# Turning gathered expert rows by a transposing DMA and a joining copy on ScalarE, in place of TensorE's transposes

## The chip, the cores and the metric

The kernel runs on one core of one Trainium2 chip. The metric is the device time of one execution in microseconds (us). Instructions run on TensorE (PE), VectorE (DVE), ScalarE (ACT) and GpSimd (POOL); SyncE (SP) issues most of the transfers, POOL and, after the change, ACT issue some too. All transfers run on the core's 16 DMA engines, whoever issues them.

## The reference

Eight sequences of 100 tokens (800 tokens of 512 words, float32) pass through a gated cross-attention block and then a gated mixture-of-experts block:

```
x = x + tanh(g_xattn) * attention(layernorm(x), ctx)          # 16 heads, fake-quantised q, k, v, weights
x = x + tanh(g_ffn)   * moe(layernorm(x))

moe(x): scores = softmax(x @ Wg.T)                            # 16 experts in 4 groups
        keep 2 groups, then 4 experts of them, with their scores as weights
        h_e = silu(x @ W1_e.T) * (x @ W3_e.T)                  # 352 wide
        y   = sum over the 4 chosen experts of score * h_e @ W2_e.T
        z   = the same product with 2 shared experts
        return y + z
```

The change touches only how the rows of one expert are brought into the layout that `x @ W1_e.T` and `x @ W3_e.T` need. Everything there is float32.

## The kernel before, in words

**Order of the work.** Projections and quantisation come first (to about 220 us), then 100 attention tiles (to about 604 us), the output projection with the second layer norm and the routing logits (to 644 us), and then the mixture of experts, 48 steps of 128 token rows. The first nine steps (`PRE`) and the last five (`POST`) are steps of the two shared experts, whose rows lie transposed in SBUF already (`x2_t`). Between them lies a loop of 17 pairs, 34 routed steps, each with one 128-row tile of the tokens of one expert.

**How the routed rows travel.** The normed tokens lie in `xn` (128 tokens by 512 words for each of T = 7 tiles). While PE is in the first shared steps, DVE ranks the experts and works out for each token four slots in a DRAM buffer, `expert_in`. POOL then scatters the tokens into their slots with 28 indirect transfers (line 1465), waits for all of them, and loads the first two tiles. In the loop POOL loads tile s + 2 into one of two buffers, `x_rows[:, q]` (line 1471), when that buffer has been read, and stores tile s - 2's result from `y_rows` to `expert_out` (line 1475) when DVE has copied it from PSUM. At the end each token gathers its four results.

**One routed step s on PE** (`routed` in the tensor block), in its order: wait for the expert's weights, for `s_xec` (this tile's rows are turned) and for `s_hm`; the first up product, four matmuls for W1, which the trace shows as eight passes (`up`, line 746); transposes of the previous step's hidden rows (`transpose_hidden`, line 757); the second up product for W3 (line 746), which ends in `s_h`; the transposes of the next tile's rows, s + 1 (`transpose_rows`, line 776); the down product of the previous step (`down`, line 766).

**The same step on ACT** (`routed` in the scalar block): `copy_hidden` moves the previous step's transposed hidden rows from PSUM to SBUF (line 968, PE's down product waits for it), `silu` on the first up product (line 962, DVE's gate at line 1284 waits for it), `copy_rows` moves the transposed rows of tile s + 1 to `xe_t` (line 974), which PE's next step waits for. DVE multiplies the two halves of the hidden rows (line 1284) and copies the down product to `y_rows` (line 1302).

**Weights.** Two transfers per expert, 1408 KB and 768 KB, are issued by SP (lines 493 and 494) into a ring of three slots, as soon as PE's down product of an expert's last tile has ended. Other than these SP issues nothing in the loop. No engine but SP issues a transposing transfer in this kernel; the ones there are, of 128 rows by 1536 half words (line 467) and of 128 by 2048 (line 410), belong to the attention part.

Of the kernel before, what the change touches and what calls it, by code (L numbers as in the profile page):

```python
# [7 lines left out]
def gated_xattn_moe_kernel(  # L8
# [16 lines left out]
    f32, bf16, i16 = mybir.dt.float32, mybir.dt.bfloat16, mybir.dt.int16  # L25
    u8, u16 = mybir.dt.uint8, mybir.dt.uint16
    ALU, ACT, AX = mybir.AluOpType, mybir.ActivationFunctionType, mybir.AxisListType

    P = 128
    NTOK, D = x.shape  # L30
    DC = D // P
# [4 lines left out]
    T = (NTOK + P - 1) // P  # L36
# [15 lines left out]
    MAXT = (NTOK * TOPK - E) // P + E + 1  # L52
# [7 lines left out]
    def shared_step(u):  # L60

        if u < PRE - T:
            return 0, u
        return (1, u - (PRE - T)) if u < PRE else (0, u - T)
# [22 lines left out]
    with ctx:  # L87
        def sb(name, shape, dt):
            return ctx.enter_context(nc.sbuf_tensor(name, shape, dt))

        def sem(name):
            return ctx.enter_context(nc.semaphore(name))
# [2 lines left out]
        key_parts = nc.dram_tensor("key_parts", [KPAD, H * P], bf16, kind="Internal").ap()  # L95


        expert_in = nc.dram_tensor("expert_in", [(MAXT + 1) * P, D], f32, kind="Internal").ap()
        expert_out = nc.dram_tensor("expert_out", [(MAXT + 1) * P, D], f32, kind="Internal").ap()


# [9 lines left out]
        xt = sb("xt", [P, T * D], f32)  # L111
# [7 lines left out]
        ident = sb("ident", [P, P], f32)  # L119
# [58 lines left out]
        ps = ctx.enter_context(nc.psum_tensor("ps", [P, 8, BANK], f32))  # L178
# [34 lines left out]
        def slot_for(n):  # L213
            return 0 if n == 0 else 1 + (n - 1) % RING

        x_rows = xt[:, 0:2 * D].rearrange("p (b d) -> p b d", b=2)
        xe_t = xt[:, 2 * D:4 * D].rearrange("p (b k q) -> p b k q", b=2, k=DC)
        y_rows = xt[:, 4 * D:6 * D].rearrange("p (b d) -> p b d", b=2)

        xn = arena_b[:, 0:T * D].rearrange("p (t d) -> p t d", t=T)  # L220
# [4 lines left out]
        v_fs = [v_f, xt[:, 0:KPAD]]  # L225

        x_t = xt[:, :].rearrange("p (k q) -> p k q", k=DC)
        attn = xt[:, :].rearrange("p (t d) -> p t d", t=T)

        zero_tile = xt[:, KPAD:KPAD + D]  # L230
# [30 lines left out]
        s_xn = sem("normed_ready")  # L261
# [52 lines left out]
        s_xz = sem("expert_in_zeroed")  # L314
        s_scat = [sem(f"tokens_scattered_{j}") for j in range(TOPK)]
        s_win = [sem(f"weights_in_{i}") for i in range(RING + 1)]
        s_wready = sem("expert_weights_ready")
        s_xr = [sem("expert_rows_in_0"), sem("expert_rows_in_1")]
        s_xtr = sem("expert_rows_transposes_done")
        s_xec = sem("expert_rows_transposed_copied")  # L320
        s_h = sem("up_products_done")
        s_silu = sem("silu_done")
# [16 lines left out]
        def rows_in(s, q):  # L339

            return 16 * (s // 2 + 1) if isinstance(s, int) else (s - q) * 8 + 16
# [27 lines left out]
        def tile_place(n):  # L369

            if n >= LAST:
                return LAST_PLACES[n - LAST]
            g, r = divmod(n, GT)
            return (g, None, T - 1) if r == GT - 1 else (g, g * HG + r // (T - 1), r % (T - 1))
# [11 lines left out]
        def _(sp):  # L386
            for t in range(T):
                rows = P if t < T - 1 else TAIL
# [14 lines left out]
            for i, a in enumerate(range(0, NKEY, CTX_PIECE)):  # L403
                b = min(a + CTX_PIECE, NKEY)
# [25 lines left out]
            def transpose_values(g):  # L430

                sp.wait_ge(s_vb, g + 1)
                sp.dma_start_transpose(v_q[:, :, g * P:(g + 1) * P], v_b).then_inc(s_vq, 16)
# [3 lines left out]
            for kt in range(KT):  # L437
                sp.wait_ge(s_parts, kt + 1)
                if kt < 2:
                    sp.wait_ge(s_fourth, kt + 1)  # L440
                sp.dma_start(key_parts[kt * P:(kt + 1) * P, :],
                             parts[:, (T + kt) % 2].rearrange("p h g d -> p (h g d)")).then_inc(s_kp[(T + kt) % 2], 16)
                if kt == 0:
                    sp.wait_ge(s_ztile, 1)
                for rows, a in ZEROED[len(ZEROED) * kt // KT:len(ZEROED) * (kt + 1) // KT]:
                    sp.dma_start(rows[a * P:(a + 1) * P, :], zero_tile).then_inc(s_xz, 16)
                if kt in GROUP_AT and kt < KT - 1:
                    transpose_values(GROUP_AT[kt])
            sp.wait_ge(s_kp[T % 2], 16 * ((KT + 1) // 2))
# [20 lines left out]
            for n in range(NTILE):  # L470
                g, head, t = tile_place(n)
# [52 lines left out]
            for t in range(T):  # L524
                rows = P if t < T - 1 else TAIL
# [6 lines left out]
        def _(pe):  # L532
# [210 lines left out]
            def up(src, col, q, w):  # L743

                for k in range(DC):
                    last = mm(ps[:, 1 + 2 * q + w, 0:INTER], src(k),  # L746
                              arena_a[:, bass.ds(col + (w * DC + k) * INTER, INTER)],
                              start=(k == 0), stop=(k == DC - 1))
                return last
# [17 lines left out]
                              arena_a[0:IW[c], bass.ds(col + UPC + c * D, D)], start=(c == 0), stop=(c == IC - 1))  # L767
                last.then_inc(s_y, 1)

            def transpose_rows(s, q):  # L770

                pe.wait_ge(s_xr[q], rows_in(s, q))
                if not isinstance(s, int) or s >= 1:
                    pe.wait_ge(s_xec, s)
                for k in range(DC):
                    last = nc.tensor.transpose(ps[:, 0, k * P:(k + 1) * P], x_rows[:, q, k * P:(k + 1) * P],  # L776
                                               ident[:, :])
                last.then_inc(s_xtr, 1)

            def shared(u, number, t, column_of, column_before):  # L780

                q = u % 2
                src = lambda k: x2_t[:, k, t * P:(t + 1) * P]
                if u >= 2:
                    pe.wait_ge(s_hm, number - 1)
                up(src, column_of, q, 0)
                if u:
                    transpose_hidden(number - 1, 1 - q)
                up(src, column_of, q, 1).then_inc(s_h, 1)
                if u:  # L790
                    down(number - 1, column_before, 1 - q)

            for u in range(PRE):
                part, t = shared_step(u)
                if u == POS_STEP:
                    positions()
                if u in (0, PRE - T):
                    pe.wait_ge(s_wready, part + 1)
                shared(u, u, t, part * SLOT, shared_step(max(u - 1, 0))[0] * SLOT)
            transpose_rows(0, 0)  # L800

            def column(s):

# [6 lines left out]
            def routed(s, q, col, need, col_before, look_up):  # L810

                u = PRE + s
                src = lambda k: xe_t[:, q, k, :]
                pe.wait_ge(s_wready, need)
                pe.wait_ge(s_xec, s + 1)
                pe.wait_ge(s_hm, u - 1)
                b = (PRE + q) % 2
                up(src, col, b, 0)
                found = look_up()
                transpose_hidden(u - 1, 1 - b)  # L820
                up(src, col, b, 1).then_inc(s_h, 1)
                transpose_rows(s + 1, 1 - q)
                down(u - 1, col_before, 1 - b)
                return found

# [21 lines left out]
        def _(act):  # L847
# [34 lines left out]
            for kt in range(KT):  # L882
                j = T + kt
# [76 lines left out]
            def silu(u, q):  # L960
                act.wait_ge(s_h, u + 1)
                nc.scalar.activation(h_act[:, q, 0:INTER], ps[:, 1 + 2 * q, 0:INTER], ACT.Silu).then_inc(s_silu, 1)  # L962

            def copy_hidden(u, q):

                act.wait_ge(s_htr, u + 1)
                for c in range(IC):
                    last = nc.scalar.copy(h_t[0:IW[c], q, c * P:(c + 1) * P], ps[0:IW[c], 5, c * P:(c + 1) * P])  # L968
                last.then_inc(s_ht, 1)

            def copy_rows(s, q):

                act.wait_ge(s_xtr, s + 1)
                nc.scalar.copy(xe_t[:, q, :, :], ps[:, 0, :].rearrange("p (k q) -> p k q", k=DC)).then_inc(s_xec, 1)

            act.wait_ge(s_xz, 16 * len(ZEROED))
            for u in range(PRE):
                if u:
                    copy_hidden(u - 1, (u - 1) % 2)
                silu(u, u % 2)  # L980
            copy_rows(0, 0)

            def routed(s, q):
                copy_hidden(PRE + s - 1, (PRE + q + 1) % 2)
                silu(PRE + s, (PRE + q) % 2)
                copy_rows(s + 1, 1 - q)

            act.wait_ge(s_slots, 1)
            pairs = act.value_load(n_pairs[0:1, 0:1], min_val=(MINT + 1) // 2, max_val=MAXT // 2)
# [393 lines left out]
        def _(pool):  # L1383
            p = nc.gpsimd
# [29 lines left out]
            for kt in range(KT):  # L1414
                j = T + kt
                b = j % 2
# [40 lines left out]
                                    ALU.mult).then_inc(s_wps, 1)  # L1457


            pool.wait_ge(s_rows, 1)  # L1460
            pool.wait_ge(s_xz, 16 * len(ZEROED))
            for n in range(T * TOPK):
                t, j = divmod(n, TOPK)
                rows = P if t < T - 1 else TAIL
                p.indirect_dma_start(out=expert_in, out_offset=bass.IndirectOffsetOnAxis(ap=slot_i[0:rows, j, t:t + 1], axis=0),  # L1465
                                     in_=xn[0:rows, t, :], in_offset=None).then_inc(s_scat[j], 16)
            for j in range(TOPK):
                pool.wait_ge(s_scat[j], 16 * T)

# [12 lines left out]
            def move_pair(b, first):  # L1482


                for q in range(2):
                    pool.wait_ge(s_xtr, b * 2 + q + 1)
                    load_rows(b * 2 + q + 2, q)
                    if not first:
                        store_rows(b * 2 + q - 2, q)
# [9 lines left out]
            for n in range(T * TOPK):  # L1499
                t, j = divmod(n, TOPK)  # L1500
                rows = P if t < T - 1 else TAIL
                if n >= NGATHER:
                    pool.wait_ge(s_comb, n - NGATHER + 1)
                p.indirect_dma_start(out=gathered[0:rows, n % NGATHER, :], out_offset=None, in_=expert_out,
                                     in_offset=bass.IndirectOffsetOnAxis(ap=slot_i[0:rows, j, t:t + 1], axis=0)
# [56 lines left out]
```

## Time and profile before

| | |
|---|---|
| median of 3 runs | 1052.98 us (1052.46 to 1056.87) |
| the profiled execution | 1052.83 us, its span 1051.3 us |
| PE busy | 981.4 us, 93% of the span |
| DVE, ACT, POOL busy | 638.5, 496.0, 445.8 us |
| mean granted clock of TensorE | 0.98 of full speed |
| the 34 routed steps | 717 to 992 us |

The page gives busy time by engine, the chain of work that ended last (followed back from the last instruction to what released each step), and groups of instructions by line. In a timeline row the first number is the start, the second how long the merged entry lasts, and the brackets show how long the engine had been idle before it and who ended the wait; an entry of PE ends a little after the next one starts, since its matmuls are pipelined.

### The profile page before, as it was taken

Reading aid. Unit: us, or ns where it says so; the run is one execution under the profiler, and the core shown is the slowest. Engines: PE = TensorE matmul, PEld = TensorE weight load, DVE = VectorE, ACT = ScalarE, POOL = GpSimd, SP = SyncE. Lnnn points to the kernel's source line nnn. Section 1 sums busy time; section 2 is a strip of 40 time slices with the busy share of each in tenths; the row PEclk is TensorE's granted clock in tenths of the full one; section 3 lists DMA queues with packets and bytes.
Section 4 is the critical chain, followed back from the end, with each engine's and each line's share of the span. In section 5 each row is a group of like instructions: output and inputs, shape, how many; then the busy total and the mean of one; then the engine's idle time right before and its main releaser. Section 6 shows DMA issues by size and latency. Waiting matters only on the chain.

```text
span 1051.3 us, 16610 instructions
## 1 busy us (share of the span) xinstructions
PE 981.4 (93%) x5718; PEld 497.3 (47%) x5719; DVE 638.5 (61%) x1141; ACT 496.0 (47%) x1051; POOL 445.8 (42%) x311
## 2 busy tenths in 40 slices
PE   5899999879999999999999899999999999999994
PEld 2334444324434444444444456555655665566551
DVE  4896766589999999999999755811111111111156
ACT  2023222259999999999999922111221122112210
POOL 1043333317887777677776830271111111111165
PEclk9999999989999999999999998999999999999997
DMA  8955646669888878888887644154544655643155
GB/s 312 233 188 206 211 182 206 204 145 146 144 135 132 128 139 141 138 146 143 128 144 110 101 180 171 55 193 138 182 176 179 232 185 199 234 163 142 50 162 160
DMA packets 268272, 172.45 MB, mean 164 GB/s; under 512 B 239344, under 2 KB 239344, under 8 KB 265904
## 3 DMA queue, kind: packets, MB, share of 16 engines
q1 hardware_dynamic: 258512, 140.14, 54.9%
q0 software_dynamic: 9696, 31.47, 8.8%
q8 instruction: 39, 0.64, 0.2%
q14 instruction: 25, 0.20, 0.1%
HBM read 68.67 MB, written 44.63 MB: 108 GB/s over the span
## 4 chain that ended last, share of the span: by engine, by line
PE 52%; POOL 18%; DVE 13%; issue 8%; ACT 5%; DMA 3%; SPq 0%; POOLq 0%; DVEq 0%; ACTq 0%
PE ps L746 18%; POOL arena_a L1447 14%; PE ps L766 9%; PE ps L581 6%; PE ps L598 5%; PE ps L558 5%; ACT arena_a L914 4%; DVE span_max L1128 3%; POOL expert_in L1465 2%; PE ps L683 2%; PE ps L640 2%; PE ps L776 1%; PE ps L757 1%; DVE proj_i L1072 1%; DVE amax L1066 1%
## 5 line engine op out<-in xcount | busy, mean ns | idle before, releaser
L1128 DVE TENSOR_REDUCE span_max<-ps 128x1 f32<-128x481 f32 (+2 forms) x400 | 351.4, 904 | 19.8 <-PE ps L598 11.7
L914 ACT ACTIVATE arena_a<-ps,exp_bias,q_step 128x962 uint8<-128x962 f32 (+1 forms) x288 | 329.9, 1157 | 23.3 <-DVE exp_bias L1148 12.5
L1447 POOL CAST arena_a<-arena_a 128x3072 bf16<-128x3072 uint8 x100 | 273.9, 2746 | 122.3 <-DMA arena_a<-arena_a 115.5
L598 PE MATMUL ps<-arena_a,q_t 128*128 128x481 bf16 (+1 forms) x864 | 225.4, 374 | 19.5 <-DVE span_max L1128 7.1
L746 PE MATMUL ps<-arena_a,xt 128*128 x544 | 172.2, 459 | 1.7 <-issue 1.7
L1284 DVE TENSOR_TENSOR proj_d<-ps,proj_f 128x352 f32<-128x352 f32 x48 | 25.2, 524 | 200.0 <-ACT proj_f L962 200.0
L968 ACT COPY proj_r<-ps 128x128 f32<-128x128 f32 x144 | 28.4, 270 | 224.2 <-PE ps L757 224.2
L766 PE MATMUL ps<-arena_a,proj_r 128*128 (+3 forms) x288 | 133.5, 600 | 0.7 <-ACT proj_r L968 0.7
L598 PEld LDWEIGHTS ps<-arena_a,q_t 128*128 128x128 bf16 x864 | 62.3, 98 | 150.2 <-ACT arena_a L914 71.0
L746 PEld LDWEIGHTS ps<-arena_a,xt 128*128 128x128 f32 x544 | 100.4, 190 | 61.2 <-issue 17.8
L581 PE MATMUL ps<-arena_a 128*128 128x512 f32 (+1 forms) x192 | 83.0, 578 | 6.3 <-ACT xt L877 4.0
L640 PEld LDWEIGHTS ps<-v_q,arena_a 128*128 128x128 bf16 x2400 | 75.7, 96 | 27.7 <-POOL arena_a L1447 8.9
L558 PE MATMUL ps<-arena_a 128*128 128x512 f32 x184 | 82.2, 592 | 0.0
L1471 POOL DMA_DIRECT2D xt<-expert_in x36 | 19.4, 539 | 147.7 <-PE ps L776 145.7
L640 PE MATMUL ps<-v_q,arena_a 128*128 128x32 bf16 (+1 forms) x2400 | 78.5, 178 | 3.1 <-POOL arena_a L1447 2.1
L598 PE MATMUL ps<-arena_b,q_t 128*128 128x481 bf16 (+1 forms) x288 | 74.8, 369 | 4.1 <-DVE span_max L1128 0.5
L766 PEld LDWEIGHTS ps<-arena_a,proj_r 128*128 128x128 f32 (+1 forms) x288 | 52.7, 193 | 50.6 <-issue 47.0
L746 PE MATMUL ps<-arena_a,q_t 128*128 128x352 f32 x224 | 72.7, 470 | 0.0
L889 ACT CAST parts<-proj_d 128x512 bf16<-128x512 f32 x23 | 14.2, 618 | 114.5 <-DVE proj_d L1083 114.5
L1302 DVE COPY xt<-ps 128x512 f32<-128x512 f32 x34 | 23.5, 692 | 68.9 <-PE ps L766 68.9
L1475 POOL DMA_DIRECT2D expert_out<-xt x34 | 18.5, 545 | 106.5 <-DVE xt L1302 106.5
L962 ACT ACTIVATE proj_f<-ps 128x352 f32<-128x352 f32 x48 | 22.2, 463 | 83.5 <-PE ps L746 83.5
(166 smaller groups left out, 933.1 us busy)
## 6 DMA issues: line engine op xcount, KB each, us to landing
arena_a<-in_w_up SPq DMA_DIRECT2D x18, 1408.0 KB, 6.4
arena_a<-in_w_down SPq DMA_DIRECT2D x18, 768.0 KB, 8.4
key_parts<-parts SPq DMA_DIRECT2D x23, 512.0 KB, 2.7
expert_in<-xt SPq DMA_DIRECT2D x42, 256.0 KB, 3.0
xt<-expert_in POOLq DMA_DIRECT2D x36, 256.0 KB, 3.0
expert_out<-xt POOLq DMA_DIRECT2D x34, 256.0 KB, 2.3
arena_a<-in_ctx_t SPq DMA_DIRECT2D x3, 1536.0 KB, 13.8
expert_out<-xt SPq DMA_DIRECT2D x17, 256.0 KB, 3.1
```

The lines of the kernel that those rows point to most:

```text
L558: last = mm(ps[:, 2 + j % 2, :], src, w_qkv[:, 0 if j < T else 1, k, :], start=(k == 0), stop=(k == DC - 1))
L581: last = mm(ps[:, 4 + v % 2, 0:w], w_qkv[:, 2, k, g * P:(g + 1) * P], ctx_sb[:, k, c * BANK:c * BANK + w], start=(k == 0), stop=(k == DC - 1))
L598: last = mm(ps[:, bank + b, 0:w], q_t[:, head, t * P:(t + 1) * P], k_t[head % NK][:, a:a + w], start=True, stop=True)
L640: last = mm(ps[:, OUT_BANK, 0:w], p_t[n % NPT][:, c, :], v_q[:, c, a:a + w], start=(c == 0), stop=(c == 2 * PC - 1))
L746: last = mm(ps[:, 1 + 2 * q + w, 0:INTER], src(k), arena_a[:, bass.ds(col + (w * DC + k) * INTER, INTER)], start=(k == 0), stop=(k == DC - 1))
L766: last = mm(ps[:, 6 + q, :], h_t[0:IW[c], q, c * P:(c + 1) * P], arena_a[0:IW[c], bass.ds(col + UPC + c * D, D)], start=(c == 0), stop=(c ...
L914: nc.scalar.activation(halves[:, :, a:a + w], ps[:, bank:bank + 2, 0:w], ACT.Exp, bias=exp_bias[:, n % 2:n % 2 + 1], scale=step_of, accum_ ...
L968: last = nc.scalar.copy(h_t[0:IW[c], q, c * P:(c + 1) * P], ps[0:IW[c], 5, c * P:(c + 1) * P])
L1128: v.tensor_reduce(span_max[:, n % 2, j:j + 1], ps[:, bank:bank + len(blocks), 0:w], AX.XY, ALU.max).then_inc(s_max, 1)
L1284: v.tensor_tensor(h_mul[:, q, 0:INTER], ps[:, 2 + 2 * q, 0:INTER], h_act[:, q, 0:INTER], ALU.mult).then_inc(s_hm, 1)
L1302: v.tensor_copy(y_rows[:, q, :], ps[:, 6 + (PRE + q) % 2, :]).then_inc(s_ya, 1)
L1447: p.tensor_copy(p_t[n % NPT].rearrange("p c q -> p (c q)").rearrange("p (j i) -> p j i", j=2), pt_u8[n % NT8].rearrange("p (i j) -> p j i" ...
```

## The change

The rows are scattered to DRAM as half words parted in two: POOL first copies each token tile of `xn` into `xn_halves`, the 512 low half words of each word first and the 512 high ones behind them. `expert_in` and `x_rows` are then of 1024 half words a row, the same bytes as before. A tile's rows are turned by one DMA transpose that ACT issues (128 rows by 1024 half words into eight blocks of 128 by 128, `x_turned`), and ACT then joins low and high halves again with one copy of 1024 half words a partition into `xe_t`. PE's four transposes per tile and the copy of their result are gone. ACT waits, at the head of a step, for its own last join and for the next tile's rows, issues the transposing transfer between `copy_hidden` and `silu`, and waits for it before the join. POOL's next load into a row buffer waits for the transposing transfer to have landed.

```diff
-        expert_in = nc.dram_tensor("expert_in", [(MAXT + 1) * P, D], f32, kind="Internal").ap()
+        expert_in = nc.dram_tensor("expert_in", [(MAXT + 1) * P, 2 * D], u16, kind="Internal").ap()
...
-        x_rows = xt[:, 0:2 * D].rearrange("p (b d) -> p b d", b=2)
+        x_rows = xt[:, 0:2 * D].bitcast(u16).rearrange("p (b c) -> p b c", b=2)
+        x_turned = xt[:, 6 * D:7 * D].bitcast(u16).rearrange("p (r q) -> p r q", q=P)
+        xn_halves = xt[:, :].bitcast(u16).rearrange("p (t h d) -> p t h d", t=T, h=2)
...
-            def transpose_rows(s, q):
-                pe.wait_ge(s_xr[q], rows_in(s, q))
-                if not isinstance(s, int) or s >= 1:
-                    pe.wait_ge(s_xec, s)
-                for k in range(DC):
-                    last = nc.tensor.transpose(ps[:, 0, k * P:(k + 1) * P], x_rows[:, q, k * P:(k + 1) * P],
-                                               ident[:, :])
-                last.then_inc(s_xtr, 1)
...
-            transpose_rows(0, 0)
...
                 up(src, col, b, 1).then_inc(s_h, 1)
-                transpose_rows(s + 1, 1 - q)
                 down(u - 1, col_before, 1 - b)
...
-            def copy_rows(s, q):
-                act.wait_ge(s_xtr, s + 1)
-                nc.scalar.copy(xe_t[:, q, :, :], ps[:, 0, :].rearrange("p (k q) -> p k q", k=DC)).then_inc(s_xec, 1)
+            def turn_rows(s, q):
+                act.dma_start_transpose(x_turned, x_rows[:, q, :]).then_inc(s_turn, 16)
+            def join_halves(s, q):
+                act.wait_ge(s_turn, (s + 1) * 16)
+                nc.scalar.copy(xe_t[:, q, :, :].rearrange("p k q -> p (k q)").bitcast(u16)
+                               .rearrange("p (r h) -> p r h", h=2),
+                               x_turned.rearrange("p (h k) q -> p (k q) h", h=2)).then_inc(s_xec, 1)
...
-            copy_rows(0, 0)
+            act.wait_ge(s_xr[0], rows_in(0, 0))
+            turn_rows(0, 0)
+            join_halves(0, 0)
             def routed(s, q):
+                act.wait_ge(s_xec, s + 1)
+                act.wait_ge(s_xr[1 - q], rows_in(s + 1, 1 - q))
                 copy_hidden(PRE + s - 1, (PRE + q + 1) % 2)
+                turn_rows(s + 1, 1 - q)
                 silu(PRE + s, (PRE + q) % 2)
-                copy_rows(s + 1, 1 - q)
+                join_halves(s + 1, 1 - q)
...
+            for t in range(T):
+                pool.wait_ge(s_xn, T + t + 1)
+                p.tensor_copy(xn_halves[:, t, :, :],
+                              xn[:, t, :].bitcast(u16).rearrange("p (d h) -> p h d", h=2)).then_inc(s_half, 1)
+            pool.wait_ge(s_half, T)
...
-                                     in_=xn[0:rows, t, :], in_offset=None).then_inc(s_scat[j], 16)
+                                     in_=xn_halves[0:rows, t, :, :].rearrange("p h d -> p (h d)"),
+                                     in_offset=None).then_inc(s_scat[j], 16)
...
-                    pool.wait_ge(s_xtr, b * 2 + q + 1)
+                    pool.wait_ge(s_turn, (b * 2 + q + 1) * 16)
```

## Rows read from the trace of the kernel before

**Rows 1.** The chain that ended last over 718 to 980 us, shares by line.

```profile
by line: PE ps L746 59.1%; PE ps L766 31.5%; PE ps L776 5.3%; PE ps L757 4.1%
```

**Rows 2.** Timeline of one routed step: start us, us, engine, line, operation, count, [idle before].

```profile
798.25 2.53 PE L746 MATMUL ps<-arena_a,xt 128*128 x8
...
798.51 0.33 SPq L493 DMA_DIRECT2D arena_a<-in_w_up  x1
...
799.93 0.54 POOL L1475 DMA_DIRECT2D expert_out<-xt  x1 [2.88 <-DVE xt L1302]
...
800.62 0.49 PE L757 MATMUL ps<-ident,proj_d 128*128 128x128 f32 x3
...
801.14 0.59 ACT L968 COPY proj_r<-ps 128x128 f32<-128x128 f32 x3 [4.69 <-PE ps L757]
...
803.31 0.60 PE L776 MATMUL ps<-ident,xt 128*128 128x128 f32 x4
...
803.51 0.46 ACT L962 ACTIVATE proj_f<-ps 128x352 f32<-128x352 f32 x1 [1.78 <-PE ps L746]
...
803.75 2.74 PE L766 MATMUL ps<-arena_a,proj_r 128*128 x6
...
804.60 0.54 POOL L1471 DMA_DIRECT2D xt<-expert_in  x1 [4.12 <-PE ps L776]
...
806.33 2.53 PE L746 MATMUL ps<-arena_a,xt 128*128 x8
```

**Rows 3.** Timeline at the loop's start: first rows landed, first routed step.

```profile
714.94 0.66 PE L776 MATMUL ps<-ident,xt 128*128 128x128 f32 x4 [0.33 <-DMA xt<-expert_in]
...
717.33 2.63 PE L746 MATMUL ps<-arena_a,xt 128*128 x8 [1.74 <-issue]
...
720.33 0.59 ACT L968 COPY proj_r<-ps 128x128 f32<-128x128 f32 x3 [4.11 <-PE ps L757]
```

**Rows 4.** DMA issues of the whole run: engine, operation, count, KB, median us to landing.

```profile
arena_a<-arena_a SPq DMA_TRANSPOSE x100, 3.9
...
q_t<-parts SPq DMA_TRANSPOSE x7, 4.6
...
arena_a<-in_w_down SPq DMA_DIRECT2D x18, 768.0 KB, 8.4
```

**Rows 5.** Lines 467 and 493 (the latter in the loop): ns min/median/max, starts.

```profile
L467 SPq DMA_TRANSPOSE arena_a<-arena_a x100: 1274/1433/2488, 226.0 to 602.3; - x100
...
L493 SPq DMA_DIRECT2D arena_a<-in_w_up x14: 327/328/337, 725.7 to 944.0; - x14
```

**Rows 6.** Line 1475, the store of one tile, in a step with a weight load.

```profile
DMA to landing us min/median/max: 7.3/7.3/7.3
```

**Rows 7.** Line 1475, the same store in the step after it, without one.

```profile
DMA to landing us min/median/max: 2.3/2.3/2.3
```

**Rows 8.** Groups by line and form: busy us, mean ns | idle before, releasers.

```profile
L974 ACT COPY xt<-ps 128x512 f32<-128x512 f32 x35 | 20.5, 586 | 3.1 <-PE ps L776 3.1
...
L968 ACT COPY proj_r<-ps 128x128 f32<-128x128 f32 x96 | 20.8, 269 | 224.2 <-PE ps L757 224.2
...
L1465 POOL DMA_INDIRECT expert_in<-arena_b,slot_i x28 | 26.8, 959 | 66.4 <-DVE slot_i L1263 58.2 <-issue 8.2
...
L1456 POOL TENSOR_SCALAR arena_a<-arena_a,v_step 128x512 f32<-128x512 f32 x4 | 6.3, 1564 | 0.0
```

**Rows 9.** Windows: us, busy us PE, PEld, DVE, ACT, POOL; granted clock, DMA share, GB/s.

```profile
742.00:750.00 8.00, 8.00 (x30) 4.83 (x29) 1.14 (x3) 1.61 (x5) 1.08 (x2) 1.00 0.89 324
...
1033.00:1036.00 3.00, 2.69 (x4) 1.20 (x5) 2.06 (x4) 0.26 (x2) 2.39 (x3) 0.60 0.78 264
...
714.00:718.00 4.00, 1.94 (x8) 0.91 (x7) 0.69 (x1) 0.58 (x1) 0.54 (x1) 1.00 0.40 125
```

**Rows 10.** Timeline of PE near the end: the last transposes and the last down product.

```profile
1032.08 0.55 PE L757 MATMUL ps<-ident,proj_d 128*128 128x128 f32 x3 [1.50 <-DVE proj_d L1284]
...
1033.31 4.54 PE L766 MATMUL ps<-arena_a,proj_r 128*128 128x512 f32 x6 [0.68 <-ACT proj_r L968]
```

More of the change, by code:

```diff
@@ L318, in gated_xattn_moe_kernel @@
         s_xr = [sem("expert_rows_in_0"), sem("expert_rows_in_1")]
-        s_xtr = sem("expert_rows_transposes_done")
+        s_half = sem("normed_halves_parted")
+        s_turn = sem("expert_rows_turned")
         s_xec = sem("expert_rows_transposed_copied")
@@ L445, in _ @@
                 for rows, a in ZEROED[len(ZEROED) * kt // KT:len(ZEROED) * (kt + 1) // KT]:
-                    sp.dma_start(rows[a * P:(a + 1) * P, :], zero_tile).then_inc(s_xz, 16)
+                    sp.dma_start(rows[a * P:(a + 1) * P, :],
+                                 zero_tile.bitcast(u16) if rows is expert_in else zero_tile).then_inc(s_xz, 16)
                 if kt in GROUP_AT and kt < KT - 1:
```

## The prediction

> **What bounds the kernel now.** I read the busy shares first (PE 93%), then the chain of waits that ended last, then one routed step in the timeline. From 718 to 980 us, almost the whole loop of 34 routed steps, the chain is PE alone: up products 59.1%, down products 31.5%, the row transposes 5.3%, the hidden ones 4.1% [rows 1]. Nothing else is in it. A step lasts 806.33 - 798.25 = 8.08 us [rows 2]. The four row transposes hold PE from 803.31 to 803.75, 0.44 us [rows 2]. That is all they cost; 5.3% of the chain over 8.08 us is the same 0.43. ACT has long rests in a step: 4.69 us before `copy_hidden`, 1.78 us before `silu` [rows 2].
>
> So the most that can be won in the loop is 34 x 0.44 = 15.0 us, and PE alone would then have a period of 7.64 us. Whether it is won hangs on one chain that the change makes new: start of step s, first up product, hidden transposes, `copy_hidden`, then on ACT the issue of the transposing transfer for tile s + 1, its landing, the join, and the start of step s + 1. Before, the rows' way to `xe_t` began with PE's own work after the second up product, and ran beside the down product. Now the transfer isn't issued before `copy_hidden` is done, and it must land and be joined within what is left of the step.
>
> **The change part by part.**
>
> *The head of the chain.* In a step that had begun from a wait, PE starts at 717.33 and `copy_hidden` ends at 720.33 + 0.59 = 720.92: 3.59 us [rows 3]. In the steady step it is 801.73 - 798.25 = 3.48 [rows 2]; I take 3.59, as the steps would begin from a wait. The new waits of ACT at the step's head (own join, rows of tile s + 1) cost nothing where the rows have landed: their load is issued when the transfer two tiles earlier has landed, more than a step ahead.
>
> *The turn, L, with no weight load beside it.* No transposing transfer of 256 KB is in this trace. The two nearest are 128 x 1536 half words = 384 KB in 3.9 us and 128 x 2048 = 512 KB in 4.6 us, both from issue to landing, on an SP queue [rows 4]. Their difference is 0.7 us per 128 KB; one step further down gives 3.2 us. Bounds: 2.3 us, which is what a plain store of 256 KB takes alone [rows 7], and 3.9, the 384 KB one. I take 3.2, as two rows point to it. The issue itself holds the queue of the issuing engine for 1.43 us at 384 KB [rows 5]; ACT's idle 1.78 us between `copy_hidden` and `silu` [rows 2] hides that. If it took longer, `silu` would be late, then the gate on DVE, but PE wants that only at the next step's hidden transposes.
>
> *The join, J.* A copy of 512 words on ACT takes 586 ns, one of 128 words 269 ns [rows 8]: 317 ns for 384 words, 0.83 ns per word. 1024 half words are then 586 + 512 x 0.83 = 1010 ns. Lower bound 0.59 (half words as cheap as half a word), upper 2.0 if the reading with a large stride from SBUF runs at half the pace. I take 1.01, as the rows are the same engine's. Behind the join on ACT stand the next `copy_hidden` (PE's down product waits for it) and `silu`.
>
> *Quiet steps.* 3.59 + 3.2 + 1.01 + 0.15 for three handovers = 7.95 us. That is above 7.64, so PE waits 0.3 us, yet still 0.13 below 8.08. 34 less the 14 steps with a weight load [rows 5] are 20: -2.6 us.
>
> *Steps with a weight load.* SP issues 2176 KB at 0.26 us into the step [rows 2]; the second transfer needs 8.4 us [rows 4], so the engines are full until about +9.0, with a DMA share of 0.89 over the step's 8 us [rows 9]. What that does to a small transfer issued into it is seen directly: the store of 256 KB, issued at +1.7 [rows 2], lands after 7.3 us [rows 6], at +9.0, with the weights, where it takes 2.3 us in the next step [rows 7]. The old kernel never felt this: nothing on PE's path was in flight then. The turn is issued at +3.6, in the middle of it. If it ends with the weights, L is 9.0 - 3.6 = 5.4; if it must also move its 256 KB after them (2 x 0.7 by [rows 4]), 6.8. I take 6.2, between. Outer bounds are 3.2 (undisturbed) and 5.4 + 3.2 = 8.6 (starts only when they end). Step: 3.59 + 6.2 + 1.01 + 0.15 = 10.95, +2.87 against 8.08, x 14 = +40.2 us.
>
> *The clock.* In such a step PE stands still for 10.95 - 7.64 = 3.3 us. Near the end of this kernel PE rests 1.50 us and 0.68 us with three short transposes between [rows 10]; the granted clock then shows 0.60 over three us [rows 9], which is a mix of the 1.2 and the 2.4 GHz level, and six passes of the down product last 4.54 us [rows 10], against 2.74 [rows 2]: 1.8 us lost. At the loop's start PE rests about as long and the window shows 1.00 [rows 9]. One gap of two, then; I charge half of the 14: +12.6 us. Bounds: 0 and 14 x 1.8 = 25.
>
> *Loop start.* The first rows have landed at 714.94 and PE starts at 717.33 [rows 3], held by its own transposes, the copy and register loads. The register loads now go by while the turn is in flight. New: 714.94 + 3.2 + 1.01 + 0.2 = 719.35: +2.0 us.
>
> *POOL's parting.* Seven copies of 1024 half words. The nearest POOL row is 1564 ns for 512 words [rows 8], so up to 3.1 us each, 22 in all; they begin with each token tile of the second layer norm, and POOL then waits 58.2 us for the slots [rows 8]. That wait hides them; without it they would stand in front of the scatter. A drag on DVE beside them I set at 0, at most 2 us. The 28 scatters move the same 2 KB rows: 0. Zeroing and gathering: unchanged.
>
> *POOL's order.* The load of tile s + 2 now waits for the turn, and the store behind it waits too, but the store needs a down product that ends no earlier than the step does: 0.
>
> Sum, from the profiled execution's 1052.8 (span 1051.3 and 1.5 around it; the median is 0.2 above): +2.0 - 2.6 + 40.2 + 12.6 = **1105 us**.
>
> **The rivals.**
>
> *The DMA engines share fairly (B).* The turn then gets its part of each engine beside the weights. By [rows 4] its own moving takes 2 x 0.7 = 1.4 us, doubled by a second stream: L = 3.2 + 1.4 = 4.6, the step 9.35, +1.27 x 14 = 17.8, with PE's rests at 1.7 us and the clock kept. 1052.8 + 2.0 - 2.6 + 17.8 = 1070. For it: the turn comes through another queue than the weights. Against: so does the store, and it waited 5.0 us longer [rows 6, 7]. The Trainium skill has this as a rule (DMA: Bandwidth & Descriptors, section "Queues, rings and completion order"): each DMA engine goes round robin over the queues with work, a packet at a time. The store's 7.3 us does not agree with an even share by bytes.
>
> *The turn is hidden (C, faster).* If the turn takes 2.9 us or less in every step, beside weights or not, then 3.59 + 2.9 + 1.01 + 0.15 = 7.65, PE never waits, and the loop gives 15.0 back: 1052.8 + 2.0 - 15.0 = 1040. It decides at L = 2.9. For it: the plain store's 2.3 [rows 7] and ACT's rests; against: both transposing rows [rows 4] and the busy engines [rows 9]. The Trainium skill says (Advanced Engine Details and Errata, section "X-Bar Transpose (TRN2)") that such DMAs are as fast as regular ones; by that L would be near 2.3 when quiet. No row here is of equal size.
>
> *Turn and join both dear everywhere (D).* L = 3.9, J = 2.0: quiet steps 9.64, +1.56 x 20 = 31; loaded ones 3.59 + 6.8 + 2.0 + 0.15 = 12.54, +4.46 x 14 = 62; the clock lost in every one, 25. 1052.8 + 2 + 31 + 62 + 25 = 1173. For it: a copy with a step of 512 half words is unseen here. Against: ACT's rate has no reason in these rows to halve.
>
> *Nothing to measure (E)*: L some 3.0 when quiet (-0.33 x 20 = -7) and 3.6 beside weights (+0.3 x 14 = +4): 1052.
>
> **How the numbers follow.** The forecast's mechanism (A) 0.53, B 0.19, C 0.12, D 0.10, E 0.06. Within 0.5%, 5 us, no change can be told for this kernel. Faster 0.13 (C, a little of E), same 0.06, slower 0.81. A's own range, with L beside weights from 5.4 to 7.5 and the clock from 0 to 25 us, is 1080 to 1135. The range for 8 in 10 takes in most of B and the near part of D: 1060 to 1145.
>
> **What would show it.** (1) DMA issues: a transposing row from ACT's queue, with its median near 3.2 and a longest of about 6 or more. (2) Chain: in the loop it passes from PE through ACT's `copy_hidden`, the transfer and the join, where it was PE alone. (3) Step starts: about 7.95 us apart, and 11 in those that follow a weight issue. (4) The join at 1.0 us. (5) Granted clock under 1.00 in some windows after long rests. A period of 7.64 everywhere would make the forecast wrong and C right; an L beside weights under 4.7 would make it B; a join of 2 us, D. If loaded and quiet steps were alike, the weights are not what matters, whatever the total is.

## The result, and the profile after

The changed kernel takes 1145.07 us (median of 4 runs, 1142.36 to 1148.88) against 1052.98 before: a ratio of 1.087, 95% interval 1.084 to 1.090. The profiled execution took 1142.62 us, 89.8 more than that of before. Forecast was 1105, with 1060 to 1145 as the range; the sign and the mechanism held, the size was short by 40 us. The result lies on the upper edge of that range, and above 1135, the top of what the forecast's own mechanism (A) was given. That the range reached so far was owed to rival D, which is refuted below, and so is luck.

The chain of waits that ended last, over 721 to 1050 us of the loop (its shares by line), which was PE alone before [rows 1]:

```profile
by line: PE ps L752 43.9%; DMA xt<-xt 34.4%; PE ps L772 12.3%; ACT xt L972 5.0%; PE ps L763 3.5%; issue 2.5%; ACT proj_r L962 0.1%; ACTq L960 0.0%
```

A third of it is now the transposing transfer, and 5% the join. The timeline of three steps that follow each other (start, length, engine, line) answers to [rows 2]:

```profile
800.72 2.53 PE L752 MATMUL ps<-arena_a,xt 128*128 x8
...
801.04 1.25 ACTq L967 DMA_TRANSPOSE xt<-xt  x1
801.14 0.43 ACT L962 COPY proj_r<-ps 128x128 f32<-128x128 f32 x2
...
804.15 1.16 ACT L972 COPY xt<-xt 128x1024 uint16<-128x1024 uint16 x1 [0.40 <-DMA xt<-xt]
...
805.67 2.53 PE L752 MATMUL ps<-arena_a,xt 128*128 x8
...
805.93 0.33 SPq L499 DMA_DIRECT2D arena_a<-in_w_up  x1
...
808.58 1.39 ACTq L967 DMA_TRANSPOSE xt<-xt  x1
...
817.67 1.16 ACT L972 COPY xt<-xt 128x1024 uint16<-128x1024 uint16 x1 [6.28 <-DMA xt<-xt]
...
818.97 5.01 PE L752 MATMUL ps<-arena_a,xt 128*128 x8 [5.49 <-ACT xt L972]
...
824.14 2.53 PE L752 MATMUL ps<-arena_a,xt 128*128 x8
...
829.09 2.53 PE L752 MATMUL ps<-arena_a,xt 128*128 x8
```

Read it in threes. In the quiet step the transfer is issued at 801.04, the join begins at 804.15, and PE's next step starts at 805.67 without a wait, 7.64 us after its predecessor. In the step that starts at 805.67 SP issues weights at 805.93; the transfer, issued at 808.58, holds the join back until 817.67, 9.1 us, and PE rests 5.49 us: the step lasts 13.30. In its successor the first up product takes 5.01 us instead of 2.53, so that this step lasts 10.12 us although nothing in it waits.

Two windows over that rest and what follows, columns as in [rows 9], show why:

```profile
813.60:818.90 5.30, 0.00 (x0) 0.00 (x0) 0.69 (x1) 1.16 (x1) 0.54 (x1) 0.82 0.75 103
818.90:824.00 5.10, 5.04 (x10) 2.94 (x11) 0.00 (x0) 0.00 (x0) 0.54 (x1) 0.52 0.34 103
```

The granted clock falls during the rest and is 0.52 in the window after it, nearly all at the 1.2 GHz level.

The transfer's own rows, the instruction on ACT's queue (ns min/median/max) and the time to its landing (us min/median/max), with the median of the weights' second transfer in the same kernel (8.4 in [rows 4]):

```profile
L967 ACTq DMA_TRANSPOSE xt<-xt x35: 1247/1254/1992, 716.6 to 1076.8; - x35
...
DMA to landing us min/median/max: 3.1/3.1/9.3
```

```profile
arena_a<-in_w_down SPq DMA_DIRECT2D x18, 768.0 KB, 9.3
```

And the groups of ACT's join and POOL's parting copy, mean ns of one (compare [rows 8]):

```profile
L972 ACT COPY xt<-xt 128x1024 uint16<-128x1024 uint16 x35 | 40.6, 1159 | 87.0 <-DMA xt<-xt 86.8
...
L1467 POOL COPY xt<-arena_b 128x1024 uint16<-128x1024 uint16 x7 | 7.3, 1039 | 16.6 <-DVE arena_b L1026 16.6
```

The starts of the 34 routed steps in the timeline account for the whole loss. In the following table "burst" is a step with a weight issue and "successor" the step after it.

| steps | before, us each | forecast | measured, mean | forecast total | measured total |
|---|---|---|---|---|---|
| 14 burst | 8.08 | 10.95 | 12.34 | +40.2 | +59.6 |
| 5 quiet, 14 successors, 1 first, without the clock | 8.08 | 7.95 | 7.64 | -2.6 | -8.8 |
| slow clock in the 14 successors | 0 | 0.90 | 2.34 | +12.6 | +32.8 |
| slow clock in the first step | 0 | 0 | 1.90 | 0 | +1.9 |
| start of the first routed step | 717.33 | 719.35 | 721.16 | +2.0 | +3.8 |

The measured column adds up to 89.3, of 89.8 in the profiled executions. Some 1.7 us of the last line arose ahead of the loop, where the runs differ by as much: ACT issued the first turn at 716.6, and PE had begun its first row transposes at 714.94 [rows 3].

### The profile page after: what moved, and what is told of

It reads as the page before. It is cut to its first block, busy times and chain, and to the rows that moved or that the text cites. A ratio compares the mean times of both kernels' runs of the same rounds, so it can differ in the third digit from the quotient of the medians.

```text
span 1141.1 us, 16390 instructions
## 1 busy us (share of the span) xinstructions
PE 1004.6 (88%) x5578; PEld 501.7 (44%) x5579; DVE 639.7 (56%) x1141; ACT 516.6 (45%) x1051; POOL 453.2 (40%) x318
## 4 chain that ended last, share of the span: by engine, by line
PE 54%; DVE 14%; DMA 13%; ACT 9%; POOL 6%; issue 5%; SPq 0%; DVEq 0%; POOLq 0%; ACTq 0%
PE ps L752 19%; DMA xt<-xt 10%; PE ps L604 9%; ACT arena_a L908 7%; PE ps L772 7%; PE ps L587 5%; PE ps L564 5%; POOL arena_a L1452 5%; DVE span_max L1133 5%; PE ps L646 3%; PE ps L689 2%; PE ps L763 1%; ACT xt L972 1%; DMA arena_b<-expert_out,slot_i 1%; PE ps L609 1%
## 5 line engine op out<-in xcount | busy, mean ns | idle before, releaser
L752 PE MATMUL ps<-arena_a,xt 128*128 x544 | 205.4, 528 | 68.9 <-ACT xt L972 63.5
L752 PEld LDWEIGHTS ps<-arena_a,xt 128*128 128x128 f32 x544 | 114.6, 220 | 147.1 <-issue 112.9
L1483 POOL DMA_DIRECT2D xt<-expert_in x36 | 19.4, 539 | 287.5 <-DMA xt<-xt 285.5
L772 PEld LDWEIGHTS ps<-arena_a,proj_r 128*128 128x128 f32 (+1 forms) x288 | 55.4, 193 | 57.7 <-issue 46.8
L972 ACT COPY xt<-xt 128x1024 uint16<-128x1024 uint16 x35 | 40.6, 1159 | 87.0 <-DMA xt<-xt 86.8
L587 PEld LDWEIGHTS ps<-arena_a 128*128 128x128 f32 x192 | 36.8, 194 | 50.9 <-issue 42.3
```

What stands on the lines that cost most here:

```text
L587: last = mm(ps[:, 4 + v % 2, 0:w], w_qkv[:, 2, k, g * P:(g + 1) * P], ctx_sb[:, k, c * BANK:c * BANK + w], start=(k == 0), stop=(k == DC - 1))
L752: last = mm(ps[:, 1 + 2 * q + w, 0:INTER], src(k), arena_a[:, bass.ds(col + (w * DC + k) * INTER, INTER)], start=(k == 0), stop=(k == DC - 1))
L772: last = mm(ps[:, 6 + q, :], h_t[0:IW[c], q, c * P:(c + 1) * P], arena_a[0:IW[c], bass.ds(col + UPC + c * D, D)], start=(c == 0), stop=(c ...
L972: nc.scalar.copy(xe_t[:, q, :, :].rearrange("p k q -> p (k q)").bitcast(u16) .rearrange("p (r h) -> p r h", h=2), x_turned.rearrange("p (h ...
```

## The experiments

Where an experiment gives L, it is the time from the issue of the turn to the start of its join in the burst steps, read from the timeline.

**Leave the weights out of the loop.** The routed steps then multiply by weights that already lie in the ring.

```diff
             def weights_ready(n):
-                sp.wait_ge(s_win[slot_for(n)], 32 * (1 if n == 0 else (n - 1) // RING + 1))
+                sp.wait_ge(s_win[slot_for(n)], 32)
...
-                load_weights(n)
```

> The changed kernel without the 14 pairs of weight transfers in the loop (the experts' products use weights already in the ring, so this part of the computation is left out). Theory (the turn is slow only beside weight transfers, and the slow clock comes only from the rests that this makes): all 34 turns land in about 3.1 us, every step is 7.64 us, granted clock 1.00 in the loop, total near 1042. Rival (some turns are slow by themselves or by the row loads and stores): long turns stay, total above 1090.

1045.60 us, beside 1053.04 for the kernel before. The landing of the turn (us min/median/max) and the loop's chain of waits:

```profile
DMA to landing us min/median/max: 3.1/3.1/3.2
```

```profile
by line: PE ps L751 62.5%; PE ps L771 33.1%; PE ps L762 4.4%
```

All 35 turns land in 3.1 to 3.2 us, all steps but the first last 7.64 us, PE alone is in the chain. So neither the turn nor the join costs PE anything by itself. The whole loss needs the weight transfers.

**Only one of the two weight transfers, 1408 KB or 768 KB.**

```diff
-                load_weights(n)
+                slot = slot_for(n)
+                sp.dma_start(arena_a[:, slot * SLOT:slot * SLOT + UPC], w_up[n]).then_inc(s_win[slot], 16)
```

The other kernel has the `w_down` line there instead; `weights_ready` counts 16 per load in both.

> The changed kernel with only the first weight transfer (1408 KB) of each expert in the loop; the 768 KB one is left out there. Theory (the turn lands some 2 us after the weights have ended): they end about 6 us into the step, the turn, issued at +3, lands at about +8.5, so L about 5.5, step about 10.3, total near 1090. Rival (what counts is only that the turn is issued into a busy queue, whatever its length): L stays near 7.8 and the total near 1140.

> The changed kernel with only the second weight transfer (768 KB) of each expert in the loop; the 1408 KB one is left out there. Theory: the weights have ended about 4 us into the step, L is 3.5 to 4.5, step 8 to 9 us, PE rests 1 us at most, clock kept, total near 1055. Rival (any busy queue at the issue costs the same): L near 7.8, total near 1140.

1110.24 and 1064.22 us. Landing of the turn, with 1408 KB and then with 768 KB:

```profile
DMA to landing us min/median/max: 3.1/3.1/7.5
```

```profile
DMA to landing us min/median/max: 3.1/3.1/5.7
```

The mean L in burst steps is 6.5 us with 1408 KB and 4.5 us with 768 KB, against 8.1 with both and 3.1 with none. It grows with what lies ahead of the turn, which refutes a fixed price for a busy queue. My totals were 20 and 9 us too low: L with 1408 KB was 1 us longer than expected, with 768 KB at the upper end of what I had, and in the first case the clock was lost too, after 12 of the 14 rests. With 768 KB PE rested up to 2.10 us ahead of a step, and no step after one lost more than 0.1 us.

**A plain transfer in place of the transposing one**, same bytes, same queue, same place. The rows are then not turned.

```diff
-                act.dma_start_transpose(x_turned, x_rows[:, q, :]).then_inc(s_turn, 16)
+                act.dma_start(x_turned, x_rows[:, q, :].rearrange("p (r q) -> p r q", q=P)).then_inc(s_turn, 16)
```

> The changed kernel with the transposing transfer replaced by a plain one of the same 256 KB between the same buffers on ACT's queue (rows are not turned, so the routed products are of other numbers). Theory (the wait for the weights is one of any transfer, and the transposing adds its many small packets on top): quiet L 2.2, beside weights 6 to 6.5, landing with the weights; burst steps about 11, total near 1100. Rival 1 (only transposing transfers suffer): L at most 3 beside weights, total near 1042. Rival 2 (the kind does not matter): L near 7.8, total near 1140.

1126.29 us. The instruction on ACT's queue in ns and its landing:

```profile
L967 ACTq DMA_DIRECT2D xt<-xt x35: 472/472/515, 719.3 to 1060.7; - x35
...
DMA to landing us min/median/max: 2.3/2.3/7.5
```

A plain transfer takes 2.3 us quiet and 7.2 in burst steps (mean), the transposing one 3.1 and 8.1. The burst adds 4.9 us to the one and 5.0 to the other, so the wait is one of any transfer of this size, as the store's had been before the change [rows 6, 7], and the turning adds 0.8 to 0.9 us on top, in both states. The slow clock stays, since PE's rests do (3.67 us at 764 us, then an up product of 4.17). My 1100 was too low for both: L 0.7 to 1.2 us longer than expected, and the clock, which was lost in all 14 successors.

**Issue the weights after the turn has landed.** `s_go` counts landed turns, set ahead by PRE - 3, so that it can be compared with `end_step`.

```diff
-                    sp.wait_ge(s_y, sp.value_load(end_step[0:1, e:e + 1], min_val=1, max_val=PRE + MAXT))
+                    end = sp.value_load(end_step[0:1, e:e + 1], min_val=1, max_val=PRE + MAXT)
+                    sp.wait_ge(s_y, end)
+                    sp.wait_ge(s_go, end)
...
                     pool.wait_ge(s_turn, (b * 2 + q + 1) * 16)
+                    pool.sem_inc(s_go, 1)
```

> The changed kernel with SP holding back each expert's weights until the turn of that step has landed, about 6 us later than before. Theory: the turn of the same step takes 3.1 us, but the next turn is issued 4.5 us after the weights and waits for their end, some 4.5 us further: L about 6.5 instead of 7.8, PE's rest 1.5 to 2.5 us shorter, clock lost in fewer cases; total 1105 to 1125. Rival (weights held back are late for PE, or the place in the burst does not matter): 1140 or more.

1117.41 us, ratio to before 1.059 (1.055 to 1.063). In 13 of 14 cases (the first load isn't held back) the next turn is issued some 4.5 us after the weights instead of 2.65, and the mean L is 6.8 instead of 8.1. The landings lie 11.2 and 10.8 us (means) after the weights' issue, and 1.1 and 0.9 us behind the landing of the second weight transfer: the turn lands a little behind the weights at either place in the burst. The total is as expected, the clock isn't: it was lost after 13 of the 14 rests, which still were 2.9 us and more.

**Fill PE's rests, to price the clock by itself.** One more up product per routed step, its result not used, first behind the down product, then ahead of it.

```diff
                 up(src, col, b, 1).then_inc(s_h, 1)
                 down(u - 1, col_before, 1 - b)
+                for k in range(DC):
+                    mm(ps[:, 0, 0:INTER], src(k), arena_a[:, bass.ds(col + k * INTER, INTER)],
+                       start=(k == 0), stop=(k == DC - 1))
```

> The changed kernel with one more up product per routed step (into an unused bank, result not used), behind the down product and ahead of the wait for the joined rows: PE's rest of 4 to 5.5 us in a burst step shrinks by 2.4 us. Theory (the slow clock after the rests comes from the length of PE's rest): most first up products after a rest run at full clock (2.5 instead of 5.0 us), burst step plus its successor about 2.3 us shorter each, quiet steps 2.0 us longer; total near 1145 + 20 x 2.4 - 14 x 2.3 = 1160. Rival (the clock falls after any rest there): 1145 + 48 = 1193.

1131.40 us: PE does 2.37 us more in each of 34 steps, and the kernel is 13.7 us faster than without. This was more than either theory said, and the timeline showed a second cause. The weights are released by the down product, which now ended before the filler, so they were issued 5.0 us ahead of the turn and L fell to 6.1. The kernel therefore changed two things, and I ran the other order:

> As the kernel with one more up product per step behind the down product, but with it ahead of the down product, so that the weights are issued at the same place of the step as in the changed kernel (2.65 us ahead of the turn, not 5.0). Theory: L stays at 8.1 in burst steps, which last about 12.5 us as before, of which PE rests 2.5 instead of 4.9; the first up product after them runs at full clock (2.5 us) in most cases, the successors last 10.0 us; pairs 22.5, quiet steps 10.0; total near 1160. Rival (the clock falls after a rest of 2.5 us too): up products of 4.3 to 5.0 us after the rests, successors 12.2 us, total near 1190.

1148.79 us. Here the weights are issued 2.65 us ahead of the turn again. A burst step and its successor, PE and the two queues:

```profile
755.17 2.53 PE L752 MATMUL ps<-arena_a,xt 128*128 x8
755.43 0.33 SPq L499 DMA_DIRECT2D arena_a<-in_w_up  x1
...
758.19 1.41 ACTq L970 DMA_TRANSPOSE xt<-xt  x1
...
767.06 2.63 PE L752 MATMUL ps<-arena_a,xt 128*128 x8 [1.71 <-ACT xt L975]
...
777.16 2.53 PE L752 MATMUL ps<-arena_a,xt 128*128 x8
```

PE's rest is 1.71 us, and the first up product behind it takes 2.63 us, at full clock. The step lasts 11.89, the successor 10.10 us, which is its 10.01 of work and next to nothing for the clock; the mean granted clock of the run is 0.979, against 0.948. PE waited 20.7 us for the join in 14 such rests, none over 1.7 us, where the changed kernel had 63.5 us in 14, from 3.5 to 5.7 us. So the transfers alone don't cost the 2.34 us of the changed kernel's successors; the long rests do. The filler adds work as well as shortening the rests, but the kernel with 768 KB in the loop has no filler, and it too kept the clock, at rests up to 2.10 us. L was 7.4 here rather than 8.1, and that is most of why 1160 was too high. The weights' second transfer landed at +9.4 instead of +10.1, and the turn 0.9 us behind it as before; why the weights were earlier no run shows.

**The parting copies alone, in the kernel before**, result not used.

```diff
+            for t in range(T):
+                pool.wait_ge(s_xn, T + t + 1)
+                p.tensor_copy(xn_halves[:, t, :, :],
+                              xn[:, t, :].bitcast(u16).rearrange("p (d h) -> p h d", h=2)).then_inc(s_half, 1)
+            pool.wait_ge(s_half, T)
```

> The kernel before with POOL's seven parting copies added and their result not used. Theory (they lie in POOL's 58 us wait): the same time within 0.3%, 1053. Rival (they slow DVE or PE in the second layer norm, where the changed kernel's loop began 1.2 us later): +1 to +3 us.

1055.97 us, ratio 1.0007 (0.9989 to 1.0024): no cost that can be measured.

**Issue the turn a step earlier.** Tile s + 2 is turned in step s, into the other of two buffers (the second in a part of `arena_b` that is idle then), each with a semaphore of its own.

```diff
+        x_turned = [a.bitcast(u16).rearrange("p (r q) -> p r q", q=P) for a in (xt[:, 6 * D:7 * D], arena_b[:, 4096:4608])]
...
             turn_rows(0, 0)
+            act.wait_ge(s_xr[1], rows_in(1, 1))
+            turn_rows(1, 1)
             join_halves(0, 0)
...
                 act.wait_ge(s_xec, s + 1)
-                act.wait_ge(s_xr[1 - q], rows_in(s + 1, 1 - q))
+                act.wait_ge(s_xr[q], rows_in(s + 2, q))
                 copy_hidden(PRE + s - 1, (PRE + q + 1) % 2)
-                turn_rows(s + 1, 1 - q)
+                turn_rows(s + 2, q)
                 silu(PRE + s, (PRE + q) % 2)
                 join_halves(s + 1, 1 - q)
...
-                    pool.wait_ge(s_turn, (b * 2 + q + 1) * 16)
+                    pool.wait_ge(s_turn[q], rows_in(b * 2 + q, q))
```

> The turn of tile s + 2 instead of s + 1 is issued in step s, into one of two buffers, so that it has a whole step more before its join. Theory (only the distance between issue and join is missing; the turn beside weights needs up to 9.3 us and would now have 7.64 + 4): all steps 7.64 us, clock 1.00, total 1052.98 - 15 + 5 at the loop's start, near 1043, faster than the kernel before by 0.7 to 1.2%. Rival 1 (the burst is now met by another wait: the row load behind the late turn, awaited at the head of the next step but one): burst pairs lose 1 to 4 us, total 1055 to 1100. Rival 2 (transfers steal bandwidth from the weights so that these are late): PE waits for weights, total above 1060.

1045.35 us, ratio to the kernel before 0.9905 (0.9881 to 0.9929), faster than both. Landing of the turns, the loop's chain of waits, and the loop as one window:

```profile
DMA to landing us min/median/max: 3.1/4.1/8.2
```

```profile
by line: PE ps L752 62.1%; PE ps L772 33.7%; PE ps L763 4.3%
```

```profile
741.00:980.00 239.00, 239.00 (x786) 139.63 (x785) 37.74 (x62) 65.56 (x158) 34.07 (x63) 1.00 0.74 225
```

The turns still need up to 8.2 us beside the weights, and nobody waits for them: PE is busy for all of 239 us, with a clock of 1.00 and steps of 7.64 us. 34 x 0.44 = 15.0 us are won, and about 5 given back at the loop's start; the profiled execution, 7.8 us ahead of that of before, had also come to the loop some 2 us later. There the first step still waits for load, turn and join in a row (15.34 us between the last hidden transposes ahead of the loop and the first in it, against 10.62 before), and the first step runs partly at the slow clock.

## Why the prediction was right in kind and short in size

**The bound and what could be won.** Right: PE alone, and 0.44 us a step. Where weights don't interfere the step is 7.64 us, which the kernel without weights in the loop and the one with the earlier turn both show.

**The head of the chain, 3.59 us: too long.** It is 2.91 (805.67 to 808.58). I let the transfer's issue follow the end of `copy_hidden`. On ACT's queue it goes out at 801.04, while two of the three copies, from 801.14 on, are still to run. The issue waits for none of their results.

**L when quiet, 3.2: right**, 3.1. The line through the two larger transposing rows [rows 4] was a good guide, though I had passed over nearer ones: the kernel before also turns 184 KB at a time out of DRAM (line 422), in 3.5 us at the median, and that would have pointed higher; the plain store's 2.3 [rows 7] was no guide, and the plain transfer in the same place took those 2.3 us. Here the Trainium skill (Advanced Engine Details and Errata, section "X-Bar Transpose (TRN2)") has transposing transfers as fast as regular ones; at 256 KB the runs show 3.1 against 2.3 us.

**The join, 1.01: close**, 1.16. The large stride was no trap. Sum of these three errors: a quiet chain of 2.91 + 3.1 + 1.16 + 0.15 = 7.32 (7.4 in the steps where the issue goes out at +3.0), under PE's 7.64, so quiet steps gained the full 0.44 and not 0.13.

**L beside weights, 6.2: the step that failed.** It is 8.1 (7.1 to 9.3). I had taken the value between "lands with the weights" (5.4) and "moves its bytes after them" (6.8), with 8.6 as the outer bound, and counted from an issue at +3.6, which puts the landing at +9.8, 0.8 us behind the weights. The real issue is at +2.9 and the landing at +11.0, so the shorter head made L longer and the step no shorter. The turn landed 0.8 to 1.0 us behind the second weight transfer in each of the 14 steps, much as forecast. The weights themselves landed later, though, at +10.1 on the mean instead of +9.1, and that I had left out. Whether the turn delays them, or the new places of POOL's load and store in the step, no run separates. In all, with a join 0.15 us longer, the burst steps last 12.34 us instead of 10.95, 19.4 us of the 40 that were missing. The plain transfer landed at 2.9 + 7.2 = +10.1, 0.9 us earlier, as it does when quiet.

Where the extra 5.0 us go can be read from the packets. These are the rows of ACT's queue, q10 (packets, MB, share of the engines' time), from the issue of the quiet turn to its join, 801.04 to 804.15, and over the first 5 us of the turn beside weights, 808.58 to 813.58:

```profile
q10 hardware_dynamic: 1056, 0.26, 44.5%
...
q10 hardware_dynamic: 31, 0.01, 0.7%
```

The first packet of a quiet turn starts 1.2 us after the issue; beside both weight transfers it starts 4.0 to 4.7 us after it, in all 14 steps. So some 3 of the 5.0 us pass before the turn has moved a byte, and 2 while it moves beside the last of the weights. With 1408 KB alone the first packet starts after 3.3 us, with 768 KB alone after 1.5 (means). What holds it back no run shows.

**The clock, half of 14 gaps at 1.8: also too small**, 14 of 14 at 2.34 us, another 20.2 us of the missing. My two examples had rests of 2.1 and 2.2 us in all [rows 3, 10], at the margin; at rests of 3.5 to 5.7 us the clock fell every time, at rests up to 1.7 us, in the kernel with the filler ahead of the down product, it was kept. The kernels without filler fill the gap: in the loop every rest of 2.9 us or more was followed by a loss, of 1.5 to 3.2 us, and of 11 rests between 1.8 and 2.8 us six were. The measured 32.8 us also lie above my upper bound of 25. Half of a pair of examples is no estimate once the expected gap is longer than both. It was also an error that compounds: a longer L makes each rest longer, so the clock term should have been tied to the burst term.

**B (fair share, 1070)** is refuted, by the amounts that scale with the weights' bytes and by the plain copy. By the rule of the Trainium skill (DMA: Bandwidth & Descriptors, section "Queues, rings and completion order") that each engine goes round robin over its queues packet by packet, I would have expected a 256 KB transfer among 2176 KB to be out early. In the changed kernel its first packet came 4.0 us after the issue or later, and it landed 0.9 us behind the weights on the mean. Once it had started it did move beside them, with half of its packets done before the weights' last. The runs show the late start, and don't test how an engine takes turns. **C (hidden, 1040)** failed in the changed kernel but is what the loop becomes when the wait is moved, 1045. **D** is refuted: neither turn nor join is dear when quiet. **The other steps**: POOL's copies took 1.04 us each, against my upper bound of 3.1, and are hidden, as forecast. The loop's start was +2.2 by its own chain (3.1 + 1.16 and handovers in place of 2.4), plus 1.9 for the clock in the first step, which I had not charged.

## What to carry to other kernels

A transfer that is put on the critical path must be priced in the traffic of the stage, not alone: read what the existing small transfers cost there in the steps with and without bulk loads, and take the full time to the end of the bulk as its price. If it can't be moved out of the bulk's way, issue it one step earlier with a second buffer; the same transfer then cost nothing, and its sign turned from +8.7% to -0.95%. And when a forecast contains long rests of TensorE, charge the slow clock in every one of them: here a rest of 2.9 us or more cost itself and 1.5 to 3.2 us besides.

## What the runs showed of the hardware that I had not expected

- A DMA of 256 KB issued on ACT's queue 2.65, 4.5 or 5.0 us after 2176 KB on SP's landed 10.8, 11.2 and 11.1 us (means) after the latter's issue: the place of its issue hardly moved its end.
- The issue of a 256 KB transposing transfer holds ACT's queue for 1.25 us, of a plain one for 0.47 us, and it can go out while earlier copies of ACT are still running.
- More work on TensorE made the kernel faster: 34 useless up products, 80 us of PE time, took 13.7 us off in one run. Two things changed with them, the clock and the earlier issue of the weights relative to the turn, and the run doesn't part their shares.
- In burst steps the DMA engines are busy with little to show near the end, one microsecond each of the step above (columns as in [rows 9]). The share rises above that of full traffic while the bytes fall to a fraction:

```profile
813.00:814.00 1.00, 0.48 (x2) 0.00 (x0) 0.39 (x1) 0.00 (x0) 0.00 (x0) 1.00 1.02 404
815.00:816.00 1.00, 0.00 (x0) 0.00 (x0) 0.00 (x0) 0.00 (x0) 0.00 (x0) 1.00 1.20 62
```

  What fills the second one is the turn, by the row of ACT's queue for it (815 to 816 us):

```profile
q10 hardware_dynamic: 51, 0.01, 108.4%
```

  Its packets of 256 bytes last 340 ns each there (mean), against 21 ns in the quiet step. Why they do isn't shown.
